# Mean terms of two tiles in one VectorE instruction, and new instruction orders, in a fused attention and FFN kernel

## The reference

```python
# x, ctx: (32, 128, 512); mask: (32, 128); w1: (2048, 512); w2: (512, 2048)
def xattn(h, m, mask):                       # h = layernorm(x)
    scores = einsum('bsd,bmd->bsm', h, m) / sqrt(512)
    scores = where(mask[:, None, :], scores, -1e30)
    return einsum('bsm,bmd->bsd', softmax(scores), m)
def bitlinear(x, w, b):                      # rms norm, rows rounded to 8 bit, w to -1, 0, 1
    xq = act_quant(rms_norm(x)); wq = weight_quant(w)
    return einsum('bsd,od->bso', xq, wq) + b
def ffn(x):
    h = gelu(silu(bitlinear(x, w1, b1)))
    return bitlinear(layer_norm(h, ln_g, ln_b), w2, b2)
x = x + xattn(layernorm(x), ctx, mask)
x = x + ffn(layernorm(x))
```

## Time and profile before

| | us |
|---|---|
| runs (3) | 419.42 median, 418.55 to 420.19 |
| the profiled execution | 418.72, span 416.8 |
| busy: PE, DVE, ACT, POOL | 380.0, 366.0, 381.7, 270.1 |
| PE clock granted, mean | 0.987 |

### The profile page before, as it was taken

The page is one execution under the profiler, slowest core; times in us unless marked ns, Lnnn a source line. Parts: engine busy times, 40 slices in busy tenths (PEclk is TensorE's granted clock), DMA queues, the critical chain, the costliest instruction groups (busy, mean ns, idle before and its releaser), DMA issues.

```text
span 416.8 us, 6814 instructions
## 1 busy us (share of the span) xinstructions
PE 380.0 (91%) x1878; PEld 202.8 (49%) x1878; DVE 366.0 (88%) x571; ACT 381.7 (92%) x517; POOL 270.1 (65%) x373
## 2 busy tenths in 40 slices
PE   3889888788999999999999999999999987899896
PEld 2576444444555544544555455554545432444342
DVE  5378589999999989999999999989998689999992
ACT  2597999999999999999999999999999999999960
POOL 6368588764787738664875569485368855477930
PEclk9999998999999999999999999999999996999999
DMA  7999991556665695658568765694754423083585
GB/s 290 412 366 320 393 289 39 176 131 143 196 172 119 177 225 158 157 164 197 150 168 239 201 171 147 201 218 102 187 133 94 91 63 63 2 201 102 90 213 128
DMA packets 108853, 73.87 MB, mean 177 GB/s; under 512 B 87048, under 2 KB 87056, under 8 KB 107536
## 3 DMA queue, kind: packets, MB, share of 16 engines
q1 hardware_dynamic: 108816, 73.43, 64.7%
HBM read 44.05 MB, written 8.39 MB: 126 GB/s over the span
## 4 chain that ended last, share of the span: by engine, by line
issue 23%; PE 22%; ACT 21%; DVE 19%; POOL 9%; DMA 4%; DVEq 0%; SPq 0%; POOLq 0%; ACTq 0%
ACT junk_v L1210 6%; DVE hid L1979 6%; PE z L623 6%; PE acc L648 5%; DVE hid L1970 5%; ACT hid L1205 4%; ACT hid L1199 4%; PE ba L573 3%; DMA xT<-in_xT_dram 3%; POOL hid L1616 3%; PE ba L584 2%; DVE am L1984 2%; PE z L628 2%; POOL rstd L1605 2%; PE bb L598 2%
## 5 line engine op out<-in xcount | busy, mean ns | idle before, releaser
L623 PE MATMUL z<-w1q,q1T 128*128 128x512 f16 x512 | 122.6, 383 | 3.9 <-ACT hid L1199 3.9
L648 PE MATMUL acc<-w2q,q2T 128*128 128x512 f16 x512 | 117.4, 379 | 1.2 <-DMA q2T<-hid 1.2
L1979 DVE SCALAR_TENSOR_TENSOR hid<-hid,rstd,beta 128x2048 f32<-128x2048 f32 x32 | 76.7, 2400 | 5.9 <-POOL rstd L1605 5.5
L623 PEld LDWEIGHTS z<-w1q,q1T 128*128 128x128 f16 x512 | 49.4, 98 | 65.1 <-ACT hid L1199 10.7
L1970 DVE SCALAR_TENSOR_TENSOR hid<-hid,nmu,gain 128x2048 f32<-128x2048 f32 x32 | 79.3, 2477 | 0.4 <-POOL nmu L1597 0.3
L648 PEld LDWEIGHTS acc<-w2q,q2T 128*128 128x128 f16 x512 | 49.8, 98 | 59.0 <-DMA q2T<-hid 2.0
L1984 DVE TENSOR_REDUCE am<-hid 128x1 f32<-128x2049 f32 x32 | 72.5, 2269 | 0.1
L1199 ACT ACTIVATE hid<-z,fac 128x1024 f32<-128x1024 f32 x64 | 70.7, 1118 | 0.8 <-PE z L628 0.5
L1221 ACT ACTIVATE junk_l<-hid 128x2050 bf16<-128x2050 f32 x32 | 61.1, 1910 | 3.7 <-DVE hid L1979 3.4
L1616 POOL TENSOR_SCALAR hid<-hid,kq 128x2048 f16<-128x2048 f32 x30 | 60.9, 2031 | 4.6 <-DVE kq L1991 3.0
L1210 ACT ACTIVATE junk_v<-hid,gsum 128x2048 bf16<-128x2048 f32 x32 | 63.7, 1990 | 0.1
(11 more groups left out here) (105 smaller groups left out, 569.4 us busy)
## 6 DMA issues: line engine op xcount, KB each, us to landing
ctxT<-in_ctxT_dram SPq DMA_DIRECT2D x32, 256.0 KB, 3.6
xs<-in_x_dram SPq DMA_DIRECT2D x32, 256.0 KB, 3.5
xT<-in_xT_dram SPq DMA_DIRECT2D x32, 256.0 KB, 3.7
ctx<-in_ctx_dram SPq DMA_DIRECT2D x32, 256.0 KB, 3.5
out_dram<-xs SPq DMA_DIRECT2D x32, 256.0 KB, 2.9
hid<-in_w1T_dram SPq DMA_DIRECT2D x4, 1024.0 KB, 9.4
hid<-in_w2T_dram SPq DMA_DIRECT2D x4, 1024.0 KB, 7.4
gain<-in_g_dram SPq DMA_DIRECT2D x1, 1024.0 KB, 10.5
```

What stands on the lines that cost most here:

```text
L623: pe.matmul(z_ps[h][:, c * CH:(c + 1) * CH], q1T[:, t % 4, k, :], w1q[:, k, f0:f0 + CH], start=(k == 0), stop=False)
L648: mm = pe.matmul(a, q2T[:, t % 2, c, :], w2q[:, c, :], start=False, stop=(c == FC - 1))
L1979: dve.scalar_tensor_tensor(out=hh, in0=hh, scalar=rstd[:, t:t + 1], in1=beta[:, :], op0=ALU.mult, op1=ALU.add).then_inc(s_l, 1)
```

## The change

ScalarE's `mean_term(t)` goes. VectorE gets `mean_terms(t)`, once for each pair: one multiplication of the 256 column sums by the two row means, each spread over 128 columns, into two neighbouring tiles of `corr`; it counts `s_corr` up by two. The numbers are the same.

```diff
@@ ScalarE
-            def mean_term(t):
-
-                act.wait_ge(s_csp, t // 2 + 1)
-                act.wait_ge(s_mv1, t + 1)
-                wait(act, s_centred, t - CR + 1)
-                act.activation(corr[:, t % CR, :], csum_ps[:, t % 2 * P:(t % 2 + 1) * P], ACT.Identity,
-                               scale=mv1[:, t, 0:1]).then_inc(s_corr, 1)
-
@@ VectorE
+            def mean_terms(t):
+
+                dve.wait_ge(s_csp, t // 2 + 1)
+                dve.wait_ge(s_mv1, t + 2)
+                wait(dve, s_centred, t - CR + 2)
+                dve.tensor_tensor(corr[:, t % CR:t % CR + 2, :], csum_ps.rearrange("p (a m) -> p a m", a=2),
+                                  mv1[:, t:t + 2, 0:1].to_broadcast((P, 2, P)), ALU.mult).then_inc(s_corr, 2)
```

SyncE, the start, the old list and the new one:

```diff
+            load_ctxT(0)
+            load_b2()
+            load_ctxT(1)
+            load_b1()
             load_mask(0)
-            load_ctxT(0)
+            load_w1(0)
             load_x(0)
-            load_ctxT(1)
+            load_ctxT(2)
+            load_x(1)
+            load_x(2)
             load_xT(0)
-            load_x(1)
-            load_w1(0)
-            load_mask(1)
+            load_xT(1)
             load_ctx(0)
             load_ctx(1)
-            load_x(2)
-            load_b2()
-            load_ctxT(2)
+            load_x(3)
+            load_x(4)
             load_ctxT(3)
-            load_b1()
-            load_xT(1)
-            load_x(3)
+            load_x(5)
+            load_x(6)
             load_w1(1)
+            load_w1(2)
             load_xT(2)
-            load_w1(2)
+            load_xT(3)
             load_w1(3)
-            load_xT(3)
+            load_xT(4)
             load_ctxT(4)
-            load_x(4)
+            load_ctxT(5)
             load_ctx(2)
-            load_xT(4)
+            load_mask(1)
+            load_mask(2)
```

TensorE, from the first products to product 4, new list:

```diff
+            first_product(3, 1)
             pe.wait_ge(s_turn, 8)
+            readout(6)
             scores(9)
             pe.wait_ge(s_silu[1], 4)
+            warm(21)
+            warm(22)
+            warm(23)
+            readout(7)
+            warm(24)
+            pe.wait_ge(s_centred, 10)
+            column_sums(10)
             turn_factors(4)
+            warm(25)
+            warm(26)
+            first_product(4, 0)
+            turn_factors(5)
             pe.wait_ge(s_x1, 8)
             turn_probs(8)
```

TensorE and VectorE, the middle, new lists (pairs 16 and 24; the lines that stay and the new ones):

```diff
@@ TensorE
+            pe.wait_ge(s_centred, 16)
+            column_sums(16)
+            second_product(4, 1)
+            second_product(5, 0)
+            first_product(10, 0)
             pe.wait_ge(s_x1, 14)
             turn_probs(14)
+            pe.wait_ge(s_corr, 18)
+            scores(16)
...
             pe.wait_ge(s_centred, 24)
             column_sums(24)
+            turn_probs(23)
             first_product(18, 1)
+            pe.wait_ge(s_corr, 26)
+            scores(24)
@@ VectorE
             q2_scale(6, 2)
+            output(4)
+            mean_terms(16)
+            prob_sum(14)
+            x1_absmax(12)
+            x1_absmax(13)
+            z_scale(12, 2)
+            prob_sum(15)
             q1_scale(12, 2)
+            gained(8)
             out_scale(6, 2)
+            invert_factors(12, 2)
+            output(5)
             normed(8)
...
             prob_sum(23)
+            z_scale(20, 2)
+            mean_terms(24)
+            norm_absmax(15)
+            q2_scale(14, 2)
+            normed(16)
             out_scale(14, 2)
+            x_stats(27)
+            softmax(24)
```

The end, ScalarE, VectorE and TensorE, new lists:

```diff
@@ ScalarE
             silu(31, 0)
             silu(31, 1)
             gelu(31)
+            square_l(30)
             variance(31)
             round_half1(30)
             square_l(31)
             round_half1(31)
@@ VectorE
             q2_scale(30, 1)
             copy_factors(34)
             copy_factors(35)
             normed(31)
             out_scale(30, 1)
+            round_half0(30)
             invert_factors(36, 1)
             norm_absmax(31)
+            output(28)
+            q2_scale(31, 1)
+            out_scale(31, 1)
+            round_half0(31)
+            invert_factors(37, 1)
             copy_factors(36)
             output(29)
             copy_factors(37)
             output(30)
@@ TensorE
+            warm(36)
+            pe.wait_ge(s_o, 27)
             turn_factors(34)
+            pe.wait_ge(s_o, 28)
             turn_factors(35)
             second_product(28, 0)
             second_product(28, 1)
             second_product(29, 0)
             second_product(29, 1)
+            pe.wait_ge(s_o, 29)
             turn_factors(36)
             second_product(30, 0)
+            pe.wait_ge(s_o, 30)
+            turn_factors(37)
             second_product(30, 1)
             second_product(31, 0)
             second_product(31, 1)
```

1730 lines of the change are left out of this document (815 added, 915 removed).

## The result

The changed kernel takes 420.36 us (median of 19 runs), the kernel before 419.42: ratio 1.0029, 95% interval 1.0016 to 1.0041. One of the 19 runs was a slow one, 673.1 us at a granted clock of 0.558, and the ratio leaves it out. The forecast was 414.3. The time lies inside the range (408.3 to 423.5), but the change made nothing faster: it is 0.3% slower, within the 0.5% that count as no change.

What follows compares the result with a forecast made beforehand. ScalarE was taken to set the pace, with TensorE and VectorE nearly level. The profiled run's 418.7 - 7.0 + 2.3 + 0.8 - 0.5 gave 414.3 us, range 408.3 to 423.5.

Steps and rivals of the forecast that it cites:

- What leaves ScalarE: ScalarE's list: 26 mean terms on the bound at 0.27 us of pace each, 7.0 us saved (6.5 to 9.5).
- The hand-over: Path through bank ba, TensorE waiting at the mask matmul: a third of the gain given back, +2.3 us (0 to 7.0).
- The start: Up to the first silu: w1's last quarter queued behind more loads, +0.8 us (-1 to +3).
- The end: Last tiles: w2 by quarters, halves and order of squares move, -0.5 us (-1 to +2).
- What comes to VectorE: VectorE: 16 mean_terms of 0.42 us, 5.6 us of pace, costed at nothing because VectorE's idle time covers them.
- Extra filler: TensorE: 37 warm calls for 20, costed at nothing, or 0.65 us each where a wait isn't there.
- the hole that I left out of the sum: TensorE after 341 us: stood 3.74 us, then slow matmuls; three fillers may give 1.7 us back, not counted.
- TensorE stands at VectorE's mean terms: Rival, mask matmul: mean_terms come late, TensorE waits over 1.5 us per pair and sets the pace; 423.0 us, chance 0.20.
- The gain is eaten: Rival, steady state: ScalarE gets shorter but TensorE or the chain through ba keeps 23.3 us; 419.0 us, chance 0.17.
- The start slips: Rival, start: the full 2.6 us delay of w1, and w2 behind it; 416.5 us, chance 0.08.
- my mark of loads 22.8 to 23.0 us apart: ScalarE: table loads of silu would stand 22.8 to 23.0 us apart if the forecast held.

Runs made afterwards that it cites:

- e3_op_only: The kernel before with only the mean terms moved from ScalarE's list to VectorE's, all other orders old; 423.17 us.
- e4_op_back: The changed kernel with the mean terms moved back from VectorE's list to ScalarE's, all other orders as changed; 434.05 us.
- e5_tail: The changed kernel with every engine's work behind about 346 us in the kernel before's relative order; 418.06 us, ratio 0.9973 to the kernel before.
- e9_less_fill: The changed kernel with 17 of TensorE's 37 fillers taken away; 421.98 us, ratio 1.0066 to the kernel before.
- e13_gained_later: The changed kernel with VectorE's gained(31) moved from ahead of output(27) to behind copy_factors(35); 422.96 us.

## Why the prediction failed, term by term

More than one term failed. What leaves ScalarE was priced right; the three terms for the new orders each slipped by about 2 us the same way: the hand-over gave back 4.3 us for my 2.3, the start cost 3.2 for my 0.8, the end cost 1.4 where I had it gain 0.5.

**What leaves ScalarE (7.0 us): right.** Between the first and the last load, from each instruction's start to the next one's, the 26 mean terms had cost 6.76 us in the trace of before, 0.260 each. Whole durations (0.365 us) would have given 9.5. For the same reason ScalarE's busy time did not fall by the 9 to 11 us that I named as a mark: overlapping instructions count once. That leaves 8.3 for all 32; why it fell by 6.8 is said under the hand-over.

**What comes to VectorE (0.42 us each, at no cost): duration right, cover true only with the new orders.** 0.415 us measured, 0.33 to the next start. The Trainium skill (VectorE: DVE Perf Modes, the errata section) gave an estimate of 0.39; the trace is 6% above it. In the old orders the same 16 instructions cost 4.2 us (e3_op_only).

**The hand-over (2.3 us): the step that failed in the middle.** The 6.76 us turned into 2.46 between the first and the last load, so 4.3 were given back. I had looked for them at TensorE's mask matmul; there the waits fell. ScalarE's own waits grew, busy time of both kernels from 60 to 350 us, before and then changed:

```profile
60.00:350.00 290.00, 272.70 (x1318) 143.53 (x1318) 271.05 (x411) 286.89 (x393) 193.97 (x248) 0.98 0.61 154
```
```profile
60.00:350.00 290.00, 276.55 (x1352) 148.52 (x1373) 270.98 (x424) 284.67 (x371) 199.52 (x250) 1.00 0.62 155
```

Its idle time went from 3.1 to 5.3 us, 2.2 more, but its waits for other engines grew only from 1.6 to 2.5. Most of the 4.3 us stands where ScalarE waits for itself. ScalarE of the changed kernel, in order of time:

```profile
267.98 0.19 ACT L1119 ACTIVATION_READ_ACCUMULATOR junk_x<-xc 128x1 f32 x1
268.26 0.63 ACT L1119 ACTIVATE junk_x<-xc 128x514 bf16<-128x514 f32 x1
268.79 0.19 ACT L1119 ACTIVATION_READ_ACCUMULATOR junk_x<-xc 128x1 f32 x1
268.89 0.26 ACT L1111 ACTIVATE probT<-bb 128x128 f32<-128x128 f32 x1
```

Behind the first read it takes 0.28 us to the next start, behind the second 0.10. The first is followed by a pass of its own kind, and square_x1, variance and square_l each wait for their forerunner's count (`wait(act, s_sq2, t)` and the like), because all calls of one kind write the same scratch tile. gelu behind gelu (12 times) and exp behind exp (9) have no such wait and follow after 0.09. Between the first and the last load the old order has 2 pairs with the wait, the new one 21 (12 of square_x1, 5 of variance, 4 of square_l): 19 more at 0.19 us are 3.6 us, half of it as small gaps and half as overlap that is lost, which is why busy time fell by 6.8 and not by 8.3. ScalarE's standing behind silu is 0.7 more; the other differences cancel. I had checked that the order of silu, gelu and exp was unchanged, and not what stands between them. No run sets these pairs apart, so how much of the 3.6 us would come through in the time is not shown. e4_op_back has 20 of the pairs, some 3.4 of the 5.9 us that the new order costs there; e3_op_only has 3, and its loss is in waits for other engines.

Below these sizes stands the wrong assumption, shown by the two-by-two table: an order laid for one division of work isn't neutral. The new one costs 5.9 us where ScalarE keeps the operation, and the move earns 7.3 in it.

**The start (0.8 us): mis-sized.** 3.2 us in the trace of the changed kernel, just over my bound of +3; with the spread of the kernels that share this start, 2.2 to 3.2. The page's chain shows the link that I had judged harmless. Chain of the changed kernel, in order of time (start, us, what):

```profile
14.37 0.96 PE ba L573 x8
...
15.35 0.33 SPq L231
...
15.72 12.15 DMA hid<-in_w1T_dram
```

I wrote that the first scores come at 11 to 12 us, long before the queue is free. They came at 14.37 to 15.33: x(0) and x(1) landed at 11.1 and 12.4 us behind w1's first block, the mean terms ended at 13.86, and fillers ahead of the scores ran to 14.3. The scores held SyncE and with it w1's last request, 5.3 us later than in the kernel before (15.72 for 10.39); the block landed at 27.87, not 25.3, 5.0 us late where my bound was 2.6. The expectation that undoing this link would undo the delay didn't hold: behind it stood w2's first block, a mask, ctx(3) and xT(3), one as late as the next.

**The end (-0.5 us): wrong in sign.** +1.4 us, undone by the old order (e5_tail). I had weighed variance(31) and round_half0. The page's chain of the changed kernel puts it on VectorE: normed(30) is 1.15 us longer beside GpSimd's rounding, and gained(31) stands ahead of output(27), which TensorE needs. The sum had no term for either; that these two are the whole of it is read from one chain and not tested. GpSimd's small steps last as long as VectorE's two-input instruction beside them, and I read their durations as GpSimd's own; but the kernel before has such a step too, 2.14 us at 385.35, on its own chain, with TensorE standing 0.83 us behind it, so it doesn't make the difference.

**Extra filler (nothing): wrong.** By e9_less_fill it is worth 1.6 us, with the reservations above, and the hole that I left out of the sum (1.7 us at 341 us) did close, while another opened ahead of 385.55 us.

**The rivals.** "TensorE stands at VectorE's mean terms" fell: 2.0 us of waits in all, 0.12 per pair where it needed 1.5. "The gain is eaten" (419.0) was nearest in time, with its mark half true: ScalarE's idle grew by a third of what its work shrank. "The start slips" (416.5) was right in its mechanism, and it came together with a longer end, which no case of mine did. I had let the terms vary one at a time. One reading under the rivals was off as well: 23.3 us a pair was the mean of three intervals between silu loads, which stand 19.07 to 25.43 us apart in the trace of before. From the second load to the last but one the mean is 22.65 us before and 22.25 after. So TensorE's room was about 0.8 us per pair and not 1.5, and my mark of loads 22.8 to 23.0 us apart could tell nothing.

The sum with measured terms: 418.7 - 6.8 + 4.3 + 3.2 + 1.4 = 420.8, against a profiled run of 421.3 and a median of 420.36. The 4.3 is what the middle lacks to the 6.8, so the sum closes by the way it is cut; it shows where the time went, and not why.

## What to carry to other kernels

When a change moves an operation and lays the orders of all engines anew, price the orders as a change of their own, with a bound of the size of the gain; cut the span into start, middle and end and let all three slip in one case. Repair a transfer-bound start as a whole: taking one late transfer away only shows the next, and engines' lists and the list of requests have to be moved together. A saving on the pacing engine is its distance from start to start, not its duration, and what a new order sets side by side on that engine has a distance of its own.

## What the hardware showed that I had not expected

- A GpSimd instruction of 12 columns or of one takes 0.2 us alone and 1.90 to 2.16 us when it starts beside VectorE's 2.34 us instruction of two inputs; it ends within 0.1 us of VectorE's (17 of 17 such steps in the changed kernel's trace). Moving VectorE's instruction moved the delay to GpSimd's next step (e13_gained_later). It also goes the other way: VectorE's normed took 3.48 us instead of 2.33 where GpSimd's rounding of 2048 columns had started first.
- On ScalarE an instruction starts 0.09 us behind the start of the accumulator read ahead of it; where the kernel makes it wait for that pass to finish, it is 0.28 (21 pairs in the changed kernel, 0.276 to 0.296).
- Behind the first silu load the profiled executions repeat to 0.03 us: 328.40 to 328.43 us from the second load to the last in seven kernels that share the middle, though their first loads lie between 40.3 and 46.4 us. In these traces only the start and the end differ.
- Fillers of TensorE that stand in waits cost nothing in the traced execution (every boundary within 0.1 us without 17 of them). The runs without them are 1.6 us slower, at mean granted clocks of 0.988 to 0.996 instead of 0.992 to 1.000.
